# The expert layers of a decoder kernel: TensorE's and ScalarE's programs written out, and the next expert's rows transposed through the other PSUM bank

## The reference

```python
C = max(math.ceil(CAPACITY_FACTOR * N / E), 1)          # 1.5 * 4096 / 8 = 768 slots
pos = jnp.take_along_axis(jnp.cumsum(onehot, axis=0), chosen_e[:, None], axis=1)[:, 0] - 1.0
kept = pos < C
buf = jnp.zeros((E, C, D)).at[chosen_e, pos_c].add(x_flat * kept[:, None])
h = jax.nn.gelu(jnp.einsum('ecd,edf->ecf', buf, w1) + b1[:, None, :], approximate=False)
eo = jnp.einsum('ecf,efd->ecd', h, w2) + b2[:, None, :]
y = eo[chosen_e, pos_c] * (chosen_p * kept)[:, None]
x = _layernorm(x + y)
```

## Time and profile before

| | us |
|---|---|
| median of 3 runs | 3785.6 (3783.69 to 3785.71) |
| the profiled execution | 3778.94 |
| its span, first to last instruction | 3777.2 |
| expert part, first matmul of e0 to the end | 2783.6 to 3777.2 |
| TensorE's busy time | 3470.1, 92% |
| VectorE's | 2519.5, 67% |

### The profile page before, as it was taken

One profiled execution on the slowest core, in us unless ns is written; L12 is line 12 of the kernel. 1 busy time (PEld: TensorE's weight loads), 2 busy tenths in 40 slices (PEclk: granted clock), 3 DMA queues, 4 the chain that ended last, 5 costly groups with the idle time before them and its releaser, 6 DMA issues. The chain is left out here.

```text
span 3777.2 us, 51836 instructions
## 1 busy us (share of the span) xinstructions
PE 3470.1 (92%) x18133; PEld 2274.6 (60%) x18134; DVE 2519.5 (67%) x4522; ACT 1754.4 (46%) x3098; POOL 2045.9 (54%) x1031
## 2 busy tenths in 40 slices
PE   7999999999999999999999858899869889899985
PEld 5455455455454554554544336788758778788874
DVE  6777777777777777777777336788634755466566
ACT  2555555555555555555555533343323433343343
POOL 2789898888988898888898820011110100110112
PEclk9999999999999999999999878999879999999998
DMA  6321322313122223223110032222132422232332
GB/s 219 95 62 55 93 63 66 98 48 97 57 65 85 66 67 91 64 66 99 48 40 12 7 98 74 81 82 77 65 114 71 136 88 97 95 104 100 118 117 99
DMA packets 190735, 309.76 MB, mean 82 GB/s; under 512 B 25609, under 2 KB 72329, under 8 KB 190490
## 3 DMA queue, kind: packets, MB, share of 16 engines
q1 hardware_dynamic: 164330, 238.58, 20.3%
q0 software_dynamic: 15072, 45.89, 3.5%
q10 hardware_dynamic: 11088, 22.02, 1.7%
HBM read 197.23 MB, written 61.33 MB: 68 GB/s over the span
## 5 line engine op out<-in xcount | busy, mean ns | idle before, releaser
L463 DVE TENSOR_REDUCE sa_part_max<-sa_mx 128x1 f32<-128x512 f32 x2048 | 1281.9, 680 | 541.5 <-PE sa_mx L574 537.4
L426 ACT ACTIVATE sa_prob<-sa_sc 128x512 f32<-128x512 f32 x2048 | 1122.0, 595 | 822.5 <-PE sa_sc L620 780.8
L247 POOL TENSOR_TENSOR sa_quad_sum<-sa_quad_sum,sa_prob 128x1024 f32<-128x1024 f32 x512 | 1207.6, 2404 | 7.7 <-ACT sa_prob L426 7.7
L574 PE MATMUL sa_mx<-sa_k_stack,sa_q_stack 96*128 96x512 f32 x2048 | 967.2, 474 | 27.1 <-DVE sa_part_max L463 15.8
L620 PE MATMUL sa_sc<-sa_q_stack,sa_k_stack 98*128 98x512 f32 x2048 | 864.6, 424 | 8.2 <-ACT sa_prob L426 8.2
L247 POOL TENSOR_TENSOR sa_quad_sum<-sa_prob 128x1024 f32<-128x1024 f32 x256 | 616.1, 2429 | 256.1 <-ACT sa_prob L426 256.1
L574 PEld LDWEIGHTS sa_mx<-sa_k_stack,sa_q_stack 96*128 96x128 f32 x2048 | 389.4, 190 | 377.1 <-issue 205.0
L620 PEld LDWEIGHTS sa_sc<-sa_q_stack,sa_k_stack 98*128 98x128 f32 x2048 | 389.1, 190 | 318.8 <-ACT sa_prob L426 273.6
L1856 PE MATMUL ex_h<-ex_xT,ex_w 128*128 128x384 f32 (+2 forms) x2688 | 467.6, 330 | 81.9 <-issue 35.0
L1856 PEld LDWEIGHTS ex_h<-ex_xT,ex_w 128*128 128x128 f32 x2688 | 450.7, 196 | 106.4 <-issue 77.8
L589 PE MATMUL sa_pv<-sa_prob,sa_v 128*32 128x512 f32 x4096 | 501.9, 608 | 0.7 <-ACT sa_prob L426 0.7
(11 more groups left out here) (201 smaller groups left out, 3397.1 us busy)
## 6 DMA issues: line engine op xcount, KB each, us to landing
ex_w_in<-in_L_ffn_w_dram SPq DMA_DIRECT2D x130, 512.0 KB, 4.3
sa_xT<-xT SPq DMA_DIRECT2D x57, 1024.0 KB, 5.1
sa_q_stack<-sa_hilo SPq DMA_DIRECT2D x372, 64.0 KB, 2.0
sa_k_stack<-sa_hilo SPq DMA_DIRECT2D x360, 64.0 KB, 2.0
ex_xg<-rows POOLq DMA_DIRECT2D x54, 256.0 KB, 3.2
rows<-sa_empty SPq DMA_DIRECT2D x48, 257.0 KB, 3.8
ex_rows<-rows POOLq DMA_DIRECT2D x8, 1542.0 KB, 7.5
sa_prob<-in_x_dram ACTq DMA_DIRECT2D x8, 1024.0 KB, 7.4
```

What stands on the lines that cost most here:

```text
L247: pool.tensor_tensor(quad_sum[:, i % 2, heads, :], so_far, prob[:, k, heads, :], ALU.add).then_inc(quad_ready, 1)
L426: act.activation(prob[:, kt % 4, j, :], sc[n % 2][:, :], ACT.Exp, scale=SCALE).then_inc(prob_ready, 1)
L463: dve.reduce_max(part_max[:, q, j, k:k + 1], mx[n % 3][:, :], AX_X).then_inc(max_read, 1)
L574: pe.matmul(mx[n % 3][:, :], q_stack[0:QK, j, at:at + P], k_stack[0:QK, g // NQ % 2, j, k * BANK:(k + 1) * BANK], start=True, stop=True).t ...
```

## The change

1. TensorE's loops over pairs of experts and over quads are gone: sixteen steps of eight experts in four variants stand one after the other. The branch on the count stays.
2. ScalarE's loop is gone: 128 steps are written out, and their semaphore values are constants.
3. The next rows are transposed at j = 0 and j = 2 instead of 0 and 1, behind the second layer and not inside it, into `h_bank[1]`, after both GELUs of the step (`h_ready`). The wait for VectorE's split moves from the beginning of the next first layer to its second half; where there is only one half, to its last matmul.
4. VectorE splits at j = 0 and j = 2 accordingly. For the last expert nothing is loaded, transposed or split.

```diff
@@ GpSimd
-                    pool.wait_ge(x_mm, done)
-                    if k > 0 or e > 0:
-                        pool.wait_ge(gathered, done * 16)
-                    load_tiles((e + 1) % E, 2 * k, 2)
+                    if e + 1 < E:
+                        pool.wait_ge(x_mm, done)
+                        if k > 0 or e > 0:
+                            pool.wait_ge(gathered, done * 16)
+                        load_tiles(e + 1, 2 * k, 2)
@@ ScalarE
-            with act.Fori(0, E * QUADS) as eq:
-                n = act.snap(eq * 4)
-                n2 = act.snap(eq * 8)
-                for j in range(4):
+            for step in range(E * STEPS):
+                q, j = divmod(step, 4)
...
@@ VectorE
-                    if q > 0 and j < 2:
-                        split_x(e + 1, 2 * q - 2 + j, 1 - par, h_bank[0])
+                    if q > 0 and j % 2 == 0 and e + 1 < E:
+                        split_x(e + 1, 2 * q - 2 + j // 2, 1 - par, h_bank[1])
@@ TensorE, first_layer
-                pe.wait_ge(w1_ready, n + j + 1 + FREE)
-                if split is not None:
-                    pe.wait_ge(x_ready, split)
...
+                    last_half = tiles * P <= (half + 1) * HALF
+                    if half == 1 and rows_left is not None:
+                        pe.wait_ge(x_ready, rows_left)
+                    for part, (pw, px) in enumerate(PARTS):
                         for k in range(KC):
+                            if half == 0 and last_half and part == 2 and k == KC - 1 and rows_left is not None:
+
+                                pe.wait_ge(x_ready, rows_left)
...
@@ TensorE, expert
+            def next_rows(e, i, row):
+
+                pe.wait_ge(h_ready, 2 * (e * STEPS + i) + 2)
+                if row % 2 == 0:
+                    pe.wait_ge(gathered, ((e + 1) * TS + row + 2) * 16)
+                transpose_rows(h_bank[1], xg[:, row % 2, :])
+
+            def expert(e, tiles):
+                for i in range(STEPS):
+                    q, j = divmod(i, 4)
+                    rows_left = None
+                    if q > 0 and j % 2 == 1 and e + 1 < E:
+                        rows_left = (e + 1) * TS + 2 * q - 2 + j // 2 + 1
+                    first_layer(e, i, tiles, rows_left)
+                    if i == 1 and e > 0:
                         pe.wait_ge(out_ready, e * TS)
...
+                    if i >= 1:
+                        second_layer(e, i - 1, tiles)
+                    if q > 0 and j % 2 == 0 and e + 1 < E:
+                        next_rows(e, i, 2 * q - 2 + j // 2)
+                second_layer(e, STEPS - 1, tiles)
...
-            with pe.Fori(0, E // 2) as pair:
-                for par in range(2):
-                    e = pe.snap(pair * 2 + par)
-                    count = pe.value_load(a.counts[0:1, bass.ds(e, 1)], min_val=0, max_val=z.TOK)
-                    fewest(count, e, pe.snap(e * STEPS), pe.snap(e * (2 * STEPS)), par, VARIANTS)
+            for e in range(E):
+                count = pe.value_load(a.counts[0:1, e:e + 1], min_val=0, max_val=z.TOK)
+                fewest(count, e, VARIANTS)
```

More of the change, by code:

```diff
@@ new lines, in first_layer, with second_layer @@
+                    last.then_inc(h_mm, 2 if half == 0 and last_half else 1)
+            def second_layer(e, i, tiles):
+                step = e * STEPS + i
+                pe.wait_ge(w2_ready, step + 1 + FREE)
+                pe.wait_ge(hT_ready, 2 * step + 2 + 2 * FREE)
+                for t in range(tiles):
+                    for part, (ph, pw) in enumerate(PARTS):
+                        last = pe.matmul(acc[t][:, :], hT[:, i % 2, ph, t * P:(t + 1) * P], w2[:, i % 2, pw, :],
+                                         start=(i == 0 and part == 0), stop=(i == STEPS - 1 and part == 2))
+                last.then_inc(o_mm, 1)
```

74 lines of the change are left out of this document (23 added, 51 removed).

## The result

| | us |
|---|---|
| before, median of 4 runs | 3785.65 (3783.69 to 3788.78) |
| changed, median of 4 runs | 3717.95 (3713.39 to 3722.76) |
| ratio | 0.9824 (0.9811 to 0.9837) |
| changed, the profiled execution | 3720.95, span 3719.2 |
| its expert part, first matmul of e0 to the end | 2787.0 to 3719.2 |

What follows compares the result with a forecast made beforehand. TensorE, busy 92% of the span, was taken as the bound, losing only its own time and waits. Gains 13.4 + 4.8 + 10.9 + 2.4 + 11.9 + 18.8 - 3 = 59.2 us from 3785.6 gave 3726 us, range 3713 to 3750.

Steps and rivals of the forecast that it cites:

- part 1: Ends of experts: TensorE's three jumps back and loop-end register work go, less 3.5 us for one exit; gain 13.4 us.
- part 4: Second half of the next first layer: new wait for VectorE's split, nearly a tie; 3 us lost, between 0 and 9.
- part 2: Starts of experts: ScalarE's table loads that delay a GELU on which TensorE waits go; gain 4.8 us.
- part 3: Quads, transposes moved: gains of 10.9 us (4 tiles), 2.4 (5 tiles), 11.9 and 18.8 (3 tiles), none with 6 tiles.
- part 5: TensorE's written-out code: up to 46 more blocks fetched, nothing charged; ends 0 and 23 us lost.
- Rival (b): Ends of experts: longer copies and new targets make remaining jumps dearer, taking back 13.4 us; gain 46, 3740 us; chance 0.10.
- rival (a): At 36 transposes the split is late by one VectorE instruction; new wait costs 25 us, 3748 us; chance 0.12.
- (c): Straight code: each of 46 more blocks stops TensorE like a far jump, 166 us lost, 3893 us; chance 0.05.

Runs made afterwards that it cites:

- e0: Not a run: expert 0, the first of the kernel's eight experts, with 6 tiles; its first matmul starts the expert part, at 2787.0 us in the changed kernel.
- e6: Not a run: expert 6 of the kernel's eight experts (numbered from 0), with 4 tiles for this input.
- e7: Not a run: expert 7, the last of the kernel's eight experts, with 3 tiles; its three quads take 52.0 us in the changed kernel.
- `pe_only`: The kernel before with only TensorE's program written out, transposes and ScalarE as before: 3762.98 us, ratio 0.9951.
- `rows_late`: The changed kernel with GpSimd's 1.5 MB load of rows issued only after VectorE has added the expert's output: 3713.84 us, ratio 0.9810.
- `fixed_tiles`: The changed kernel without the count's load and branches, each expert's number of tiles written into the program: 3678.62 us, ratio 0.9721.
- `act_loop`: The changed kernel with ScalarE's loop of before, and so its table loads, put back: 3731.65 us, ratio 0.9863.
- `adds_spread`: The changed kernel with three of VectorE's six additions moved into q0 and the scaling spread: 3718.80 us, ratio 0.9830.
- the bank alone: The kernel before with only the transposes and waits moved, loops kept, the last expert still bringing rows in: 3757.63 us, ratio 0.9931.
- ScalarE alone: The kernel before with only ScalarE's loop written out, TensorE and the bank as before: 3753.13 us, ratio 0.9924.

## Why the prediction was right

The forecast was 3726 us with a range of 3713 to 3750; 3718 was measured. The sum was 59.2 us against 61.4 in the expert parts. That it came so near is partly luck, since part 1 was 2.5 us too high and the 3 us of part 4 did not come. From step to step of the two traces the 61.4 split as follows. An end is here from the last step's first layer to the next expert's start.

| term | forecast | measured |
|---|---|---|
| part 1, ends of experts | 13.4 | 10.9 |
| part 2, their first quads | 4.8 | 4.6 |
| part 3, 6-tile quads (e0, e3) | 0 | 0.4 |
| 4-tile quads (e5, e6) | 10.9 | 11.1 |
| 5-tile quads (e2, e4) | 2.4 | 3.3 |
| e1's quads | 11.9 | 12.3 |
| e7's quads | 18.8 | 18.8 |
| part 4, the new wait | -3 | 0 with 4 to 6 tiles |
| part 5, straight code | 0 | 0 |
| sum | 59.2 | 61.4 |

**Part 1** is the term that was sized too high. The step that failed is the sentence that the remaining jumps stay as they were, with 3.5 us charged for the one that had been short. e1 and e3 ended 5.2 and 6.2 us sooner, 11.4 together, of 11.6 for their two jumps back. e5 gained nothing and lost 0.3, e6 lost 0.6. Exits of e5 and e6 took 5.71 and 4.99 us, and the entry of e2 6.22 where it had been 4.87. Rival (b) had seen this coming, but by the wrong cause: code length. `pe_only` has the same length and short jumps, and `rows_late` changes one wait of GpSimd and has short jumps too. The cause is the 1.5 MB load, under way in e2's entry and with the weights held up behind it in the two exits. I also read the row of 12.5 us as VectorE's, and feared VectorE in the gap's place. Two of its three places are jumps and the third is e0's start. In the changed kernel VectorE takes nothing at these places; only without jumps do 9.1 us of it appear, at step 1. The compare-and-branch of about 108 ns that the Trainium skill gives (Advanced Engine Details and Errata, Control Flow Timing) holds for near or untaken branches, 65 to 80 ns here; the far ones took 3.4 to 6.2 us, and `fixed_tiles` puts the whole test of the count, jumps and clock, at 37 us.

**Part 2** came out at 4.6, but not expert by expert. e1's first quad gained 2.9 us: its wait for the late GELU fell from 2.13 to 0.76, as charged, and the first layer of step 1 took 2.33 us in place of 3.83, at a higher clock. e6's first quad lost 1.4. Its exit and entry left TensorE idle for 7.0 us, and this is the stretch behind (columns as in the earlier trace rows):

```profile
3503.25:3515.00 11.75, 11.75 (x51) 11.67 (x52) 3.95 (x8) 3.12 (x6) 0.00 (x0) 0.60 0.09 28
```

A mean clock of 0.60 over 11.75 us. It would be easy to say that the dearer jump costs a second time, as clock, but the same kernel measured again speaks against a rule for single starts: there e6's gap was longer, 7.7 us, and the clock behind it 0.80 over 11.8 us, and e1's step 1, behind the same wait of 0.76, took 4.18 us and not 2.33. So what e1 gained and e6 lost beyond the waits is scatter of the clock. The sum holds better: the first quads gained 4.6 us in one execution and 5.2 in the other, and against `act_loop`, where the tables are back, they are 5.5 us shorter, for the 4.8 that I charged.

**Part 3** held to 1 us in each line. For e7 my own terms give 50.2 + 1.5 = 51.7 us, and I wrote 52.0; that 52.0 was measured is chance at this size. VectorE as the bound in e1's q1 and q2 was right: I had 41 and 18.6 us, measured are 40.6 and 18.6. `adds_spread` shows it as cause, not only as a busy share: five of VectorE's operations fewer in that stretch (72 for 77) made it 3.4 us shorter. What I had not seen is which part of the change does it in the 4-tile quads. I put the waits of 4-tile quads down to the bank, and so did the bank alone; but the table loads were part of the same waits, and ScalarE alone takes 40% of them.

**Part 4** charged 3 us for the new wait, for a near tie. (It counted 30 transposes outside e1 and e7; there are 36, as in rival (a), and the charge would have been 3.6.) The split ends about 0.5 us ahead of the second half in the 4-tile step shown above, and no quad of 4 to 6 tiles waits at all. The wait does exist: 4.6 us in four places, all of them in e1, where it was already inside the 41 and 18.6 us. So rival (a), with 25 us, did not come.

**Part 5** was right, and (c) with it wrong: the fetches grew from 46 blocks and 0.75 MB to these

```profile
q8 instruction: 59, 0.97, 0.4%
```

and 6-tile quads are 34.1 us wide with TensorE busy all of it. 13 blocks came, not up to 46: the upper end of part 5 was far too high, which made (c) dearer than it could have been. I have no run that tells why; loops that fetched again what they repeated would explain it. As the Trainium skill has it (Runtime: NRT & Kernel Launch, Instruction fetch mechanics), the next code comes in while the current is executed; the 6-tile quad without a gap agrees.

**The remaining 6 us** stand between 61.4 and the 67.7 of the medians. The interval of the ratio begins just above the 61.4, at 62; the second measurement has 67.0, with an interval from 59. No run here finds a place for them in the expert part, whose sum was the same in two executions. Whether they are chance or lie ahead of e0, where the start scatters by 13 us in unchanged code, stays open.

Of what the profile was to show afterwards, nearly all came true: e2 and e4 start 5.1 and 4.7 us after the last matmul, as written, there is one table load, and the quads have their widths. The wait for `issue` fell to 18 us for the 21 written, but that row is no measure of the jumps, since 14.5 us of them stand in the row put down to VectorE.

## What to carry to other kernels

When several edits act on one chain (late GELU, transposes, split, next layer), the waits that each removes are the same ones. Price them together, or in an order: ScalarE's part was worth 29.2 us alone and 11.4 on top of the others. A data-dependent branch on the busiest engine costs its jump, what transfers of other queues add to it and the half-clock time behind the gap; work that every branch needs belongs ahead of it, and large loads away from it. Unrolling gained mostly by what it removed at the joints (jumps back, table loads), and 2.5 of the 17.6 us of `pe_only` inside the loops. And where a wait is put down to an engine, ask which instruction the semaphore's value stands for, and when that one ended.

## What the runs showed of the hardware

- A far jump of TensorE ends 1.4 to 1.6 us after a 16 KB packet of the instruction queue has come, in the changed kernel. With little else transferred the packet begins 0.9 to 1.2 us after the jump's start and the jump takes 3.4 to 4.2 us. With a load of 1.5 MB under way, or the weights queued behind it, it begins after 2.6 to 3.6 us and the jump takes 5.0 to 6.2; moving the load (`rows_late`) brought these three to 4.0 to 4.4.
- TensorE was granted half of its clock (0.50) for 4 us behind a gap of 4.7 us after full activity; taking out the test of the count, with gaps of 32.6 us, gave 37.4 us back, 24.9 of idle time and 12.4 of clock. In two executions of one kernel the clock behind the same start differed: 0.60 over 11.8 us behind a gap of 7.0 us, 0.80 behind one of 7.7.
- ScalarE's loop loaded its tables twice in each of 32 passes, 1.28 us each; the same instructions without the loop needed one load. In a chain of waits this was worth 29.2 us, with slack in the chain 11.4.
- Written-out code at a weight load and a matmul every 0.11 to 0.17 us showed no gap that a fetch would explain, in quads of 4 and 6 tiles.
